# Attention: the order of the TensorE work within a score group

## The reference

```python
qkv = hidden_states @ W_attn + b_attn
q, k, v = jnp.split(qkv, 3, axis=-1)            # 32 heads of D = 8
scores = jnp.einsum('bhqd,bhkd->bhqk', q, k) / jnp.sqrt(jnp.float32(D))
scores = jnp.where(causal, scores, MASKED_BIAS)
scores = scores + jnp.where(causal, cols - rows, 0.0) * m
probs = jax.nn.softmax(scores, axis=-1)
attn = jnp.einsum('bhqk,bhkd->bhqd', probs, v)
out = attn.transpose(0, 2, 1, 3).reshape(B, S, E) @ W_proj + b_proj
```

## Time and profile before

| | us |
|---|---|
| median of 3 runs, not profiled | 1329.46 |
| span of the profiled execution (the page gives no time around it) | 1345.1 |
| attention with scores, units 0 to 14 | about 92 to 538 |
| one unit in the steady part (303.48 to 333.10) | 29.62 |
| in that unit: PE busy, DVE busy, ACT busy | 28.92, 24.52, 21.31 |

### The profile page before, as it was taken

One profiled execution on the slowest core, in us unless ns is written; L12 is line 12 of the kernel. 1 busy time (PEld: TensorE's weight loads), 2 busy tenths in 40 slices (PEclk: granted clock), 3 DMA queues, 4 the chain that ended last, 5 costly groups with the idle time before them and its releaser, 6 DMA issues. The chain is left out here.

```text
span 1345.1 us, 32608 instructions
## 1 busy us (share of the span) xinstructions
PE 1226.9 (91%) x13048; PEld 709.8 (53%) x13080; DVE 860.2 (64%) x1737; ACT 572.0 (43%) x857; POOL 253.0 (19%) x433
## 2 busy tenths in 40 slices
PE   6889999999999999889989977996899999979998
PEld 3523333333333333265656644443788888867775
DVE  7487888887888888057222263898566766664432
ACT  3416767777767777732223204563112111112221
POOL 4400010001000100020466500224311222300000
PEclk9959999999999999999999997998899999999999
DMA  4501211111222110060242230000200000000000
GB/s 128 77 2 17 41 29 27 28 27 27 38 39 32 27 29 4 8 218 0 69 143 87 77 123 0 1 1 0 81 4 4 3 4 4 3 3 0 16 16 32
DMA packets 33836, 49.47 MB, mean 37 GB/s; under 512 B 11995, under 2 KB 22331, under 8 KB 32955
## 3 DMA queue, kind: packets, MB, share of 16 engines
q1 hardware_dynamic: 29211, 36.55, 12.1%
q0 software_dynamic: 3744, 10.23, 2.4%
q10 hardware_dynamic: 768, 1.05, 0.2%
HBM read 23.63 MB, written 9.31 MB: 24 GB/s over the span
## 5 line engine op out<-in xcount | busy, mean ns | idle before, releaser
L671 DVE TENSOR_REDUCE at_block_max<-at_p_ring 128x4 f32<-128x512 f32 x576 | 367.8, 686 | 75.1 <-PE at_p_ring L577 42.6
L648 ACT ACTIVATE at_probs<-at_p_score,abias 128x1024 f32<-128x1024 f32 (+2 forms) x320 | 318.9, 1029 | 125.1 <-PE at_p_score L607 70.6
L577 PE MATMUL at_p_ring<-kt,qt 64*128 64x128 bf16 (+3 forms) x1152 | 187.2, 284 | 15.0 <-DVE at_block_max L671 6.9
L622 PE MATMUL at_p_out<-at_probs,at_vs 128*32 128x512 f32 (+3 forms) x1536 | 165.5, 503 | 0.4 <-ACT at_probs L648 0.4
L601 PE MATMUL at_p_score<-qt,kt 64*128 64x512 bf16 (+3 forms) x768 | 146.5, 332 | 5.7 <-ACT at_probs L648 4.8
L577 PEld LDWEIGHTS at_p_ring<-kt,qt 64*128 64x128 bf16 x1152 | 69.9, 95 | 126.9 <-DVE at_block_max L671 86.6
L714 POOL TENSOR_TENSOR at_shift<-shift,at_row_max 128x16 f32<-128x16 f32 x32 | 7.1, 222 | 422.8 <-DVE at_row_max L677 422.8
L601 PEld LDWEIGHTS at_p_score<-qt,kt 64*128 64x128 bf16 x768 | 38.4, 94 | 86.7 <-ACT at_probs L648 54.4
L2098 ACT COPY rc_ta<-rc_bank 128x256 f32<-128x256 f32 x32 | 10.4, 375 | 149.8 <-PE rc_bank L1852 149.8
L2240 PE MATMUL fi_p_in<-fi_xt,w_in 128*128 128x512 f32 x128 | 62.4, 611 | 0.7 <-ACT fi_xt L2276 0.7
L607 PE MATMUL at_p_score<-anticausal,ident 128*128 128x128 bf16 (+1 forms) x384 | 62.9, 246 | 0.0
(11 more groups left out here) (346 smaller groups left out, 2155.8 us busy)
## 6 DMA issues: line engine op xcount, KB each, us to landing
qt<-qparts SPq DMA_DIRECT2D x96, 64.0 KB, 2.5
kt<-kparts SPq DMA_DIRECT2D x96, 64.0 KB, 2.5
rows<-moe_chosen SPq DMA_DIRECT2D x4, 1024.0 KB, 4.8
w_routed<-in_w_routed_dram SPq DMA_DIRECT2D x1, 2816.0 KB
x<-in_x_dram SPq DMA_DIRECT2D x4, 512.0 KB, 8.9
moe_table<-rows SPq DMA_DIRECT2D x4, 512.0 KB, 2.7
out_dram<-x SPq DMA_DIRECT2D x4, 512.0 KB, 2.9
w_down<-in_w_down_dram SPq DMA_DIRECT2D x1, 1408.0 KB
```

The source lines that it names most:

```text
L577: mm = pe.matmul(bank[:, col:col + nb * P], qt[nxt][h * ROWS:(h + 1) * ROWS, pair, t * P:(t + 1) * P], kt[nxt][h * ROWS:(h + 1) * ROWS, pa ...
L622: mm = pe.matmul(p_out[32 * h:32 * h + 32, left(k):QC], vs[(now - e[2]) % BUFS][:, key, h, :], probs[g % PROBS][:, h % 2, at:at + w], star ...
L648: act.activation(probs[g % PROBS][:, :, 0:len(pairs) * w], p_score[g % 2][:, :, 0:len(pairs) * w], ACT.Exp, bias=abias[:, c * TPB + key:c ...
L671: dve.tensor_reduce(dst, src, AX.X, ALU.max).then_inc(s["fill_used"], 1)
```

## The change

The list of a group is put together from three parts, in this order: `rows` (all products that use 64 rows: the scores, and one pair of fills of the two heads, whose products alternate between the heads block by block), `full` (products on 128 rows by 128 columns: the masks of the scores and of the diagonal fills, which become events of their own, `shift` and `out`), and `columns` (the `pv`, `take` and `max`). 18 of the 20 groups carry exactly two fills, both heads of one entry of `FILLS`; groups 5 and 19 carry none. The order of the entries is changed (`FILL_ORDER`), `out_now` moves from group 9 to group 11 and `shift 0` from 13 to 14. PE waits for both banks of a pair before its first product. The number of products, masks, transposes and reductions is the same.

```diff
-FILLS_PER_GROUP = [2, 5, 1, 1, 3, 0, 3, 0, 4, 1, 2, 1, 2, 2, 2, 1, 2, 2, 2, 0]
-EXTRA = {0: ["shift_own"], 1: ["prev"], 5: ["out_prev"], 9: ["out_now"], 13: ["shift 0"]}
+FILL_GROUPS = [(0, 1, 2, 3, 4, 6, 7, 8, 9), (10, 11, 12, 13, 14, 15, 16, 17, 18)]
+FILL_ORDER = [(0, 1, 2, 8, 3, 4, 5, 6, 7), (1, 0, 2, 3, 8, 4, 5, 6, 7)]
+EXTRA = {0: ["shift_own"], 1: ["prev"], 5: ["out_prev"], 11: ["out_now"], 14: ["shift 0"]}
...
     for g in range(NG):
-        part = []
+        rows, full, columns = [], [], []
         if "s" in kind:
-            part.append(("scores", g))
+            rows.append(("scores", g))
+            if on_diagonal(g):
+                full.append(("cover_scores", g))
+        for pair in range(2 if "m" in kind else 0):
+            if g in FILL_GROUPS[pair]:
+                at = FILL_ORDER[pair][FILL_GROUPS[pair].index(g)]
+                rows += [("fill", 1, pair, 2 * at), ("fill", 1, pair, 2 * at + 1)]
+                if at in DIAGONALS:
+                    full.append(("cover_fills", 1, pair, 2 * at))
+                if g == FILL_GROUPS[pair][-1]:
+                    columns.append(("max", pair))
...
+        ev += rows + full + columns
     return ev
...
             for n, e in enumerate(ev):
-                if in_ring(e):
+                if in_ring(e) and not (e[0] == "fill" and e[3] % 2):
                     wait_bank(pe, ev, n, u, third)
                     bank = p_ring[ring_bank(e, third)]
-                if e[0] == "fill":
+                if e[0] == "fill" and e[3] % 2 == 0:
...
+                    wait_bank(pe, ev, n + 1, u, third)
+                    banks = bank, p_ring[ring_bank(ev[n + 1], third)]
                     col = 0
                     blocks, where, _ = FILLS[at]
                     for t, b0, nb in blocks:
-                        mm = pe.matmul(bank[:, col:col + nb * P], qt[nxt][h * ROWS:(h + 1) * ROWS, pair, t * P:(t + 1) * P],
-                                       kt[nxt][h * ROWS:(h + 1) * ROWS, pair, b0 * P:(b0 + nb) * P],
-                                       start=col == 0, stop=where != "diagonal", skip_group_check=True)
+                        for h in range(2):
+                            mm = pe.matmul(banks[h][:, col:col + nb * P], qt[nxt][h * ROWS:(h + 1) * ROWS, pair, t * P:(t + 1) * P],
+                                           kt[nxt][h * ROWS:(h + 1) * ROWS, pair, b0 * P:(b0 + nb) * P],
+                                           start=col == 0, stop=where != "diagonal", skip_group_check=True)
+                            if where != "diagonal" and (t, b0, nb) == blocks[-1]:
+                                mm.then_inc(s["fill_ready"], 1)
                         col += nb * P
...
+                elif e[0] == "cover_fills":
+                    _, ahead, pair, f = e
+                    for h in range(2):
+                        pe.matmul(p_ring[ring_bank(("fill", ahead, pair, f + h), third)][:, :], ident16[:, :],
+                                  causal16[:, :, :].rearrange("p b c -> p (b c)"),
+                                  start=False, stop=True, skip_group_check=True).then_inc(s["fill_ready"], 1)
...
+                elif e[0] == "cover_scores":
```

More of the change, by code:

```diff
@@ L398, with on_diagonal @@
 PAIR_FILLS = 2 * len(FILLS)
-ROTATED = 0
+DIAGONALS = [n for n, fill in enumerate(FILLS) if fill[1] == "diagonal"]
 LOAD_GROUP = 2
-FILLS_PER_GROUP = [2, 5, 1, 1, 3, 0, 3, 0, 4, 1, 2, 1, 2, 2, 2, 1, 2, 2, 2, 0]
-assert sum(FILLS_PER_GROUP) == 2 * PAIR_FILLS
-EXTRA = {0: ["shift_own"], 1: ["prev"], 5: ["out_prev"], 9: ["out_now"], 13: ["shift 0"]}
-def slot_events(kind):
[L408 to L421, removed]
+FILL_GROUPS = [(0, 1, 2, 3, 4, 6, 7, 8, 9), (10, 11, 12, 13, 14, 15, 16, 17, 18)]
+FILL_ORDER = [(0, 1, 2, 8, 3, 4, 5, 6, 7), (1, 0, 2, 3, 8, 4, 5, 6, 7)]
+EXTRA = {0: ["shift_own"], 1: ["prev"], 5: ["out_prev"], 11: ["out_now"], 14: ["shift 0"]}
+def on_diagonal(g):
+    c, kt, _ = GROUPS[g]
+    return kt * P >= c * QC
+def slot_events(kind):
+    ev = []
     for g in range(NG):
-        part = []
+        rows, full, columns = [], [], []
         if "s" in kind:
-            part.append(("scores", g))
+            rows.append(("scores", g))
[9 more added lines that the diff above has]
+                    columns.append(("max", pair))
         for name in EXTRA.get(g, []):
@@ L428, in slot_events @@
             if what == "shift" and "m" in kind:
-                part.append((what, int(arg), 0))
+                full.append((what, int(arg), 0))
             if what == "shift_own" and "s" in kind:
-                part.append(("shift", 1, 1))
-            if what == "prev" and "p" in kind:
[L433 to L437, removed]
+                full.append(("shift", 1, 1))
+            if what == "out_prev" and "p" in kind:
+                full.append(("out", 1, 1))
+            if what == "out_now" and "s" in kind:
+                full.append(("out", 0, 0))
+            if what == "prev" and "p" in kind:
+                columns += [("pv", len(STEPS) - 1, 1), ("take", 1, 1)]
         if "s" in kind:
@@ L440, in slot_events @@
                 if last_group(k) + 2 == g:
-                    part.append(("pv", k, 0))
+                    columns.append(("pv", k, 0))
                     if k == LAST0:
[L443 to L452, removed]
+                        columns.append(("take", 0, 0))
+        ev += rows + full + columns
     return ev
@@ L468, in ring_bank @@
     full = [x for x in slot_events(FULL) if in_ring(x)]
-    return (third + (full.index(e) if e in full else e[3] - ROTATED)) % RING
+    return (third + full.index(e)) % RING
 assert sum(map(in_ring, slot_events(FULL))) % RING == 1
@@ L592, in tensor_slot @@
                     w, pairs = place(g)
-                    diag = key * P >= c * QC
                     if g in (group_of(0, 0), group_of(0, 1)):
@@ L603, in tensor_slot @@
                                            qt[now][h * ROWS:(h + 1) * ROWS, pair, (c + 1) * QC - w:(c + 1) * QC],
-                                           start=i == 0, stop=not diag, skip_group_check=True)
-                    for h in range(2 if diag else 0):
-                        over = score[:, h, 0:len(pairs) * w].rearrange("p (i w) -> p i w", w=w)[:, :, 0:P]
+                                           start=i == 0, stop=not on_diagonal(g), skip_group_check=True)
+                    if not on_diagonal(g):
+                        mm.then_inc(s["scores_ready"], 1)
+                elif e[0] == "cover_scores":
+                    g = e[1]
+                    w, pairs = place(g)
+                    for h in range(2):
+                        over = p_score[g % 2][:, h, 0:len(pairs) * w].rearrange("p (i w) -> p i w", w=w)[:, :, 0:P]
                         mm = pe.matmul(over, ident16[:, :], anticausal16[:, 0:len(pairs), :],
@@ L673, in vector_slot @@
                     pair = e[1]
-                    dve.wait_ge(s["fill_used"], ring_place(ev, n - 1, u))
+                    last = max(i for i in range(n) if ev[i][0] == "fill")
+                    dve.wait_ge(s["fill_used"], ring_place(ev, last, u))
                     dve.tensor_reduce(row_max[:, 2 * pair:2 * pair + 2, :].rearrange("p h (j e) -> p h e j", e=2),
```

9 lines of the change are left out of this document (3 added, 6 removed).

## The result

| | before | after |
|---|---|---|
| median, us | 1331.51 (4 runs) | 1368.91 (4 runs, 1368.02 to 1370.67) |
| ratio | | 1.0287 [1.0266, 1.0308] |
| span of the profiled execution | 1345.1 | 1366.2 |
| attention in it, first fill to the last `pv` | 501.3 | 538.3 |

The change costs 37.4 us. I had forecast 15.5, and the time lies outside my range. In the two profiled executions the attention differs by 37.0, though the spans differ by 21.1: behind the attention, where nothing was changed, the execution of before that was profiled took 777.8 us, and all others of this study took 760 to 767. So I set attention against attention.

A forecast was written before the change was run, and what follows sets the result against it. PE was taken to set the pace: 24.9 us own work plus 5.8 waits make a unit 30.7 against 29.62. Over 15 slots 16.5, first slot +1, first unit -2: 15.5 us, 1345; 8 in 10 for 1331 to 1361.

The forecast's parts named there:

- PE's own work: PE's products and changes of kind in a steady unit, without waits: 24.8 to 24.9 us, against a unit of 29.62 before.
- The bank waits: PE standing before pairs of fills until DVE has read earlier banks: 4.8 us a unit, plus 0.3 where pairs follow closely.
- `shift`: PE at the shift of group 0 waits for POOL's last step on the maxima: 0.38 us a unit.
- the DMA of the shift rows: PE reaches the scores of group 2 too soon for the landing of the shift: 0.3 us a unit.
- the faster rival: Only banks behind a `shift` or `out` are late: unit 27.8, time 1302, 8%; with no wait at all 24.9, 1258, 2%.
- the one within 0.5%: DVE's spacing or the latencies a tenth shorter, about 0.7 us less waiting a unit: 1335, 13%.
- first slot: The slot of fills alone, at the 1.2 GHz level: loses about 1 us, diagonal pairs winning an estimated 0.2 each.
- 15 slots with both passes: Slots that hold both passes, each unit 1.1 us longer: 16.5 us.
- the rival "the clock": Waits of 1.3 us in groups 18 to 2 bring the 1.2 GHz level, up to 1.7 us more a unit: 1370, 5%.
- a stretch like 542.70 to 546.10: Before, PE had little to do there, with waits of 0.86 and 0.72; the next 3.40 us ran at 1.2 GHz.
- The gain of 2 in the first unit: The part of the first unit at half clock gains about 2 us, as PE's own work is larger there.

The follow-up runs named there:

- the last run: The changed kernel's list reordered to leave the banks time, with each fill in the first slot waiting for its own bank; 1283.99 us, ratio 0.964.

## Why the prediction was wrong

**What bounds the kernel, and PE's own work: right.** From start to start, the steady unit of after has waits of 5.7, so PE's own work is 25.0, where I had 24.9. In the timeline above, group 16's scores and fills and group 17's scores follow without a change (218.80, 219.01), and before the fills of group 17 there are 0.95 from the last start, of which the scores are 0.22: a wait of 0.73. (The 0.57 in brackets is less, since it counts from the modelled end.)

**The bank waits: right, one by one.** Group 17: 0.70 forecast, 0.73 measured. Group 15: 1.00 and 1.03. Group 1: 0.62 and 0.60; group 12: 0.56 and 0.58; group 4: 0.50 and 0.53; group 3: 0.44 and 0.46. All waits for DVE in one unit: 5.1 forecast (4.8 + 0.3), 5.1 measured. `shift`: 0.38 and 0.40. Only the DMA of the shift rows is smaller, 0.14 instead of 0.3. The unit is 30.7 as forecast. So the faster rival is out, and so is the one within 0.5%, which needed latencies a tenth shorter.

**The step that failed: the sum had no term for the code.** Where I wrote that PE issues neither fill before both banks are free, I costed the two waits as time and not as instructions. Ahead of the loop they are 33 instructions more, and those push the loop over a block's edge. The sum of attention, taken apart by the trace:

| us | forecast | after | loop's place put back |
|---|---|---|---|
| first slot, first fill to first scores | +1 | +4.0 | +3.0 |
| three jumps back, with the clock behind them | 0 | +16.5 | 0 |
| the rest: 15 slots with both passes, first and last parts | +14.5 | +16.5 | +16.1 |
| together | +15.5 | +37.0 | +19.1 |

The last column is the run that leaves out 30 of the waits ahead of the loop, and those like them behind it. Its time, 1.0130 [1.0094, 1.0167] or 12.5 to 22.2 us over before, takes in the 15.5; that of after doesn't.

Of the 16.5, the stands are 9.4 (the row of waits). The remaining 7 go with the half clock behind each of them, 6.8 to 10.3 us long by the windows: behind the first stand, from the scores of group 0 to those of group 4 PE took 9.19 us (226.70 to 235.89), in a steady unit 6.47 (161.96 to 168.43). So the rival "the clock" came about, but not by its mechanism, and that its 1370 is near the time measured is chance: the 1.3 us of waits in groups 18 to 2 never lowered the clock in a steady unit (granted clock 1.00 in 163.46 to 194.16), and it fell behind stands of 3.0 to 3.3 us. I had looked for a stretch like 542.70 to 546.10 in the wrong place.

**Mis-sized: the first slot.** I had a plain pair at 1.35 instead of 1.2, and an estimated gain of 0.2 at each diagonal pair. The PE timeline of the run with the loop's place put back:

```profile
70.08 0.61 PE L587 MATMUL at_p_ring<-kt,qt 64*128 64x512 bf16 x2 [0.79 <-DVE at_block_max L689]
71.47 0.61 PE L587 MATMUL at_p_ring<-kt,qt 64*128 64x128 bf16 x8 [0.78 <-DVE at_block_max L689]
72.01 1.04 PE L596 MATMUL at_p_ring<-causal,ident 128*128 128x512 bf16 x2
73.40 0.60 PE L587 MATMUL at_p_ring<-kt,qt 64*128 64x512 bf16 x2 [0.36 <-DVE at_block_max L689]
75.39 0.61 PE L587 MATMUL at_p_ring<-kt,qt 64*128 64x512 bf16 x2 [1.38 <-DVE at_block_max L689]
```

A plain pair takes 1.39 (70.08 to 71.47), and a diagonal pair and the one behind it 3.92 (71.47 to 75.39) instead of two times 1.39: the pair behind a diagonal one waits for DVE too, which is still at the diagonal fills. I had looked at the gain on PE alone. In after a plain pair takes 1.46; that 0.07 goes with the second wait's own instruction, the only thing in which the two differ there. That these waits and not the order cost the time is shown by the run in which each fill waits for its own bank: 24.4 us against 25.9 before. (There the heads also go one after the other.)

**The gain of 2 in the first unit: not in after.** I had expected it from PE's own work at half clock, so that this unit would be 0.9 shorter than before (1.1 longer, less 2). From its first scores to those of the next unit it takes 33.90 us before and 35.35 in after. With the loop's place put back it takes 33.40, so 0.5 of the 0.9 is there; but in that execution the half clock ended 10.7 us into the unit, and before 13.9 (13.4 in after). How much comes from PE's work and how much from the earlier end isn't shown.

**Open.** The kernel before, moved by the same 33 places, missed once and then kept its code; after missed at each jump. Its loop is one instruction longer than the old one; whether that decides, or the time at which the code is asked for, no run here tells. Why a late jump cost 3.0 us in the mean with the old order half a block on and 5.5 with the new can be followed further, by the packets: in after two are fetched within 1.7 us of each jump's start, and so in the kernel before moved by 33, and these jumps take 4.3 to 4.9 us. Half a block on only one is, since the packet before it came some 5 us earlier (206.8 and 212.1 us, jump at 211.2), and the jumps take 3.3 to 3.8. With the shorter jumps PE stands for 1.9, 1.5 and 1.7 us instead of 3.3, 3.0 and 3.1, and the half clock lasts 6.8, 0 and 3.4 instead of 10.3, 6.8 and 6.8. That the time of the packet decides is read from these figures and wasn't tried by itself.

## What to carry to other kernels

Where a change adds waits, count the instructions too, and compare before and after the code packets of the page's part 3 and the first matmul behind each jump back: a loop near the size that stays loaded can fall out by a few instructions *ahead* of it, and it can be brought back by moving it. Where a pair of products takes two of three banks, the wait of each pair follows from the start of the product that completes the fill before, DVE's spacing and the return; worked out from rows, those sums held to 0.06 us in each group that waited. Grouping products by kind paid only after the list had been put in an order in which the banks come back in time: 26.54 us a unit instead of 30.70, with the same products on the same engines.

## What the runs showed of the hardware that was not expected

- A PE loop of 1755 or 1756 instructions stays loaded when it starts at place 785, 788 or 1041 of the program, and is loaded again when it starts at 818 (at one jump or at all three) or 912 (at all three). A late jump takes 3.3 to 4.9 us instead of 0.22, and costs 1.6 to 6.1 us with what follows. The Trainium skill, Runtime: NRT & Kernel Launch, section Instruction fetch mechanics, gives PE 128 KiB of instruction memory in blocks of 16 KiB, 256 instructions, and says that a taken branch to a page outside the current two has to fetch it first; by an estimate from that (128 / 16), eight blocks would fit. The runs agree with the blocks and the fetch, but not with the two pages: before, a jump back over the 1755 instructions of the loop, at least seven blocks, fetched nothing. The loops begin 0, 3 or 256 places behind that of before where they stay, and 33 or 127 where they don't: a loop that spills over into an eighth block is fetched again, at one jump at least, and one that fits into seven isn't. A pass of after loads 9 packets, one more than its eight blocks; if the ninth is the block behind the loop, fetched ahead, then seven blocks and that one are the eight that fit. This reading is argued, not tried.
- Stands of 3.0 to 3.3 us on PE were followed by the 1.2 GHz level for 6.8 to 10.3 us, those of 1.93 and 1.74 half a block on by 6.8 and 3.4, one of 1.52 by none, and a wait of 1.83 for a DMA (the last run) by 3.4; waits of up to 1.03 us in a unit with some 25 of work left the clock at 1.00.
- A fulfilled wait that is an instruction of its own takes PE 0.106 us (33 of them in the kernel before, moved).
